# A new order of the opening: k by arrival, the first norm on ScalarE, q in pairs, four divisions and most weight remainders on VectorE

## The chip, the cores and the metric

One core of one Trainium2 chip. The metric is the time of one execution on the device in microseconds (us); lower is better. TensorE is called PE in the profile (its weight loads PEld), VectorE DVE, ScalarE ACT, GpSimd POOL, SyncE SP.

## What is computed

A gated cross-attention block followed by a mixture of experts, in float32. Shapes: x and ctx (4, 512, 256); 16 heads of 64; a window of 65 keys; 2 shared and 16 routed experts of width 128, the best 4 routed ones counted.

```
x = x + tanh(g_xattn) * attention(layernorm(x), ctx, ctx)
x = x + tanh(g_ffn)   * experts(layernorm(x))

attention: q = rope(layernorm(x) @ wq.T); k = rope(ctx @ wk.T); v = ctx @ wv.T
           s = q k^T / 8, masked to i-64 <= j <= i; softmax(s) v; @ wo.T
experts:   gate = top 4 of softmax(x @ router.T)
           sum over experts of gate_e * gelu(x @ up_e.T) @ down_e.T
```

## The kernel before

**Products.** Each float32 operand is split into a high part in the fp32r type and a remainder (`h`, `l`); a product is three matmuls: high by high, high by remainder, remainder by high (`products`, `product`). ScalarE rounds the high part and another engine subtracts it from the source. So each 128x512 piece of weights (`("w", i)`) is loaded to `raw` (4 slots) by SyncE, rounded by ScalarE (L579, semaphore `w_hi`), and its remainder is made either by VectorE (L840, `w_lo_v`), if `i` is in `LO_ON_V`, or by GpSimd (L479, `w_lo_p`). A slot of `raw` is loaded again once both are done (`load_piece`, L338).

**Units.** The attention runs over 16 units (4 batches by 4 groups of 4 heads), `u`, and 64 heads, `c`. For a unit TensorE makes q, k and v (L1009) in one of two pairs of PSUM banks, taken in turn (`ring`): each job takes the pair of the last job but one, and waits until that has been read (`claim`, `released`). q and k are rotated: VectorE shuffles the bank into `swap` (L768) and multiplies the bank by cos (L771); GpSimd multiplies `swap` by sin (L465; L455 for both pairs at once) and adds (L467, L458). A "pair" is half of a unit's q or k, two heads. v goes out through ScalarE (L595).

**Heads.** `scores` (TensorE, L1160, two heads at a time), `score_max` (VectorE, L910), `softmax_numerator` (ScalarE, L628), `invert` (VectorE, the reciprocal of the row sums, L920), `divide` (GpSimd, L471, prob times rinv broadcast, both in SBUF), `transpose_probs` (TensorE, L1172), `copy_transposed` (ScalarE, L637), `values` for two heads (TensorE, L1191), `round_att` (ScalarE, L643) and `rest_att` (VectorE, oTl, L924). When a unit's four heads are done, ("y", u) multiplies by wo and VectorE adds the result to x (L856).

**Order.** All of it is written by hand: each engine has its own queue, a list for the opening (up to head 4) and then a loop over `steps`, one for each head from `OPENED` = 5, with the same jobs on every engine. Engines meet only through semaphores. In the opening VectorE makes the statistics of the first layer norm (L730 to L737) and norms the four tiles of x itself (`normalise_first`, L742); GpSimd makes `rstd` (L490), and only for later norms also `shift`, which ScalarE's `normalise` (L618) needs. k0 waits for both parts of ctx before each half. q of unit 0 is rotated by pairs, q of later units in one piece; VectorE, before it shuffles a q or k, waits until GpSimd is done with the whole of the last one (`joined`). The PE queue of the opening is k0, xT0 (x turned), v0, q0, k1, scores 0, q1, v1, transposes 0, scores 2, transposes 1, q2, values 0, scores 4. After the attention the experts follow with up and down products, without the parts that the change touches.

## Time and profile before

| | before |
|---|---|
| median of 3 runs | 523.23 us (522.90 to 523.24) |
| the profiled execution | 523.18 us |
| its span in the profile | 521.4 us |
| TensorE busy | 503.8 us, 97% |
| VectorE, ScalarE, GpSimd busy | 357.4, 311.1, 276.1 us |
| granted TensorE clock, mean | 0.999 |

The profile shows one execution. A line of a timeline gives start, duration, engine, source line, operation, tiles written and read, shapes, how many, and in brackets the engine's idle time before it with what ended that. Durations of neighbours on one engine overlap somewhat, so start-to-start times are used for sums. A granted clock of 1.00 is TensorE's level of 2.4 GHz.

### The profile page before, as it was taken

To read this page: it belongs to the slowest core of one execution; us is meant where nothing else is said; L and a number is where in the kernel's file an instruction comes from. 1 tells how busy PE (TensorE), PEld (TensorE's weight loads), DVE (VectorE), ACT (ScalarE), POOL (GpSimd) and SP (SyncE) were. 2 spreads that over 40 slices of the span, in tenths; PEclk is the share of its full clock that TensorE was granted. 3 is DMA by queue.
4 is the path that set the end of the run, shared out by engine and by line. 5 is a ranking of instruction groups with operands and counts; after the bars stand their busy time and mean duration, and the time that the engine had idled before them with its cause. 6 is when DMAs were issued, how large, how long until landed. Compare 5 with 4: busy or idle time off the path is not lost.

```text
span 521.4 us, 12294 instructions
## 1 busy us (share of the span) xinstructions
PE 503.8 (97%) x4394; PEld 422.2 (81%) x4394; DVE 357.4 (69%) x1150; ACT 311.1 (60%) x859; POOL 276.1 (53%) x213
## 2 busy tenths in 40 slices
PE   8888999899999999999999999999999999999996
PEld 4767798799889988888888888867887888788884
DVE  6868868558756577775967575697657665855463
ACT  3468677466676657766675794764546545544442
POOL 3989997788889778987998733541000100000000
PEclk9999999999999999999999999999999999999999
DMA  8352323111031011202221128314911491156021
GB/s 258 98 166 50 81 77 105 55 37 36 4 117 36 13 27 36 59 1 58 58 56 43 37 74 314 88 28 107 301 25 21 127 284 17 24 150 233 1 33 47
DMA packets 47723, 44.12 MB, mean 85 GB/s; under 512 B 29168, under 2 KB 31472, under 8 KB 47664
## 3 DMA queue, kind: packets, MB, share of 16 engines
q1 hardware_dynamic: 47664, 43.35, 29.2%
q8 instruction: 35, 0.57, 0.4%
q14 instruction: 24, 0.20, 0.1%
HBM read 30.62 MB, written 2.23 MB: 63 GB/s over the span
## 4 chain that ended last, share of the span: by engine, by line
PE 72%; POOL 10%; DVE 9%; issue 5%; ACT 2%; DMA 1%; SPq 0%; DVEq 0%; POOLq 0%; ACTq 0%
PE ring L1009 50%; PE psS L1009 8%; PE psO L1191 5%; PE psS L1160 4%; PE psT L1172 4%; POOL arena L465 3%; POOL arena L467 2%; POOL prob L471 2%; DVE arena L768 2%; POOL wl L479 1%; POOL arena L458 1%; DVE prob L819 1%; DMA craw<-in_ctx 1%; DVE wl L840 1%; DVE arena L910 1%
## 5 line engine op out<-in xcount | busy, mean ns | idle before, releaser
L1009 PE MATMUL ring<-xTh,wh 128*128 128x512 f32 x272 | 109.7, 403 | 3.0 <-DVE wl L840 1.4
L1009 PE MATMUL ring<-xTh,wl 128*128 128x512 f32 x272 | 106.8, 393 | 0.0
L1009 PE MATMUL ring<-xTl,wh 128*128 128x512 f32 x272 | 106.7, 392 | 0.0
L471 POOL TENSOR_TENSOR prob<-prob,rinv 128x512 f32<-128x512 f32 x64 | 68.0, 1063 | 15.5 <-DVE rinv L920 15.5
L566 ACT ACTIVATE oTh<-prob 128x512 fp32r<-128x512 f32 x64 | 40.4, 632 | 58.0 <-PE ring L1009 26.5
L827 DVE TENSOR_TENSOR oTl<-prob,oTh 128x512 fp32r<-128x512 f32 x64 | 46.3, 724 | 39.4 <-ACT oTh L566 39.1
L1009 PEld LDWEIGHTS ring<-xTh,wh 128*128 128x128 f32 x272 | 51.1, 188 | 16.6 <-issue 4.4
L819 DVE TENSOR_TENSOR prob<-sneg,arena 128x512 f32<-128x512 f32 x64 | 47.4, 740 | 21.6 <-ACT sneg L550 21.6
L637 ACT ACTIVATE pT<-psT 128x512 f32<-128x512 f32 x64 | 38.0, 593 | 40.3 <-PE psT L1172 40.3
L550 ACT ACTIVATE sneg<-ring 128x512 f32<-128x512 f32 x72 | 42.8, 595 | 32.0 <-PE ring L1009 31.9
L1009 PEld LDWEIGHTS ring<-xTh,wl 128*128 128x128 f32 x272 | 51.0, 188 | 11.3
L1009 PEld LDWEIGHTS ring<-xTl,wh 128*128 128x128 f32 x272 | 51.2, 188 | 10.6
L628 ACT ACTIVATE prob<-arena,nmax 128x128 f32<-128x128 f32 x128 | 49.8, 394 | 10.6 <-DVE nmax L910 10.6
L628 ACT ACTIVATE prob<-sneg,nmax 128x128 f32<-128x128 f32 x128 | 49.5, 391 | 9.9 <-DVE nmax L910 9.9
L467 POOL TENSOR_TENSOR arena<-arena 128x512 f32<-128x512 f32 x36 | 47.3, 1313 | 2.8
L465 POOL TENSOR_TENSOR arena<-arena,sin 128x512 f32<-128x512 f32 x36 | 47.4, 1318 | 1.3 <-DVE arena L768 1.3
L455 POOL TENSOR_TENSOR arena<-arena,sin 128x1024 f32<-128x1024 f32 x14 | 34.0, 2428 | 25.1 <-DVE arena L768 25.1
L768 DVE STREAM_SHUFFLE arena<-ring 128x512 f32<-128x512 f32 (+1 forms) x49 | 45.3, 924 | 0.2
L479 POOL TENSOR_TENSOR wl<-raw,wh 128x512 fp32r<-128x512 f32 x22 | 30.9, 1404 | 26.7 <-ACT wh L579 26.6
L1172 PE MATMUL psT<-ident,prob 128*128 128x128 f32 x256 | 39.0, 274 | 5.0 <-POOL prob L471 5.0
L490 POOL TENSOR_TENSOR rstd<-vare,mhalf 128x4 f32<-128x4 f32 x8 | 9.2, 1155 | 63.0 <-DVE vare L737 63.0
L771 DVE TENSOR_TENSOR arena<-ring,cos 128x512 f32<-128x512 f32 (+1 forms) x49 | 40.9, 835 | 0.0
(123 smaller groups left out, 1226.2 us busy)
## 6 DMA issues: line engine op xcount, KB each, us to landing
arena<-gate_scratch SPq DMA_DIRECT2D x64, 256.0 KB, 6.4
raw<-in_e SPq DMA_DIRECT2D x18, 256.0 KB, 2.7
raw<-in_w SPq DMA_DIRECT2D x16, 256.0 KB, 3.6
arena<-arena SPq DMA_DIRECT2D x16, 256.0 KB, 3.1
arena<-arena SPq DMA_DIRECT2D x16, 192.0 KB, 3.4
pT<-pT SPq DMA_DIRECT2D x96, 32.0 KB, 2.0
out<-x SPq DMA_DIRECT2D x16, 128.0 KB, 6.2
x<-in_x SPq DMA_DIRECT2D x3, 512.0 KB, 3.8
```

Source lines behind the costliest of these rows:

```text
L465: link(pool.tensor_tensor(part, part, sin[:, :], ALU.mult))
L467: pool.tensor_tensor(dst, dst, part, ALU.add).then_inc(qk_rot[i], 1)
L471: pool.tensor_tensor(prob[:, c % BUFS, :, :], prob[:, c % BUFS, :, :], rinv[:, c % BUFS, :].unsqueeze(2).to_broadcast([P, TT, P]), ALU.mul ...
L550: act.activation(act_g[:, n % 2, :], ring[0][:, n % 2, :], ACT.Gelu).then_inc(f_gelu, 1)
L566: act.activation(gated_parts(n)[0], src, ACT.Copy).then_inc(f_hi, 1)
L628: last = act.activation(prob[:, c % BUFS, t, :], sneg[c % BUFS][:, t, :], ACT.Exp, bias=nmax[:, c % 4, t:t + 1], scale=-1.0, accum_out=rsu ...
L768: dve.stream_shuffle(swap[:, i, pairs, :], part, [(lane + QUAD // 2) % QUAD for lane in range(QUAD)]).then_inc(qk_swap[i], 1)
L771: dve.tensor_tensor(dst[:, pairs, :], part, cos[:, :].unsqueeze(1).to_broadcast(part.shape), ALU.mult).then_inc(qk_mul[i], 1)
L819: dve.tensor_tensor(act_f[:, n % 4, :], act_g[:, n % 2, :], gate_bc[:, r, :], ALU.mult).then_inc(f_mul, 1)
L827: dve.tensor_tensor(lo, src, hi.bitcast(F32), ALU.subtract).then_inc(f_lo, 1)
L1009: last = pe.matmul(out, a, b, start=start and i == 0 and j == 0, stop=stop and i == n - 1 and j == 2, skip_group_check=check)
L1172: last = pe.transpose(psT[:, t, :], prob[:, c % BUFS, t, :], ident[:, :])
```

## The change

The opening's queues are rewritten; the loop over `steps` stays as it is but for three things: which weight remainders lie on VectorE, that q is rotated by pairs up to unit 2 (`SPLIT_Q`), and that head 4's reciprocal and division move into the opening.

- k0 (`first_keys`): products come in the order in which their inputs arrive: high ctx of part 0 by both halves' weights, then weights' remainder, ctx's remainder, then part 1.
- The first layer norm goes through ScalarE's `normalise` behind weight 1; `normalise_first` is gone, and GpSimd makes `shift` for it too.
- Divisions of heads 0 to 3 run on VectorE (`divide` in the vector block, new semaphore `s_norm_v`).
- Remainders of weights 1, 3, 5, 9, 11, 13, 15 go from GpSimd to VectorE, those of 2 and 6 from VectorE to GpSimd.
- VectorE waits per pair for GpSimd (`rotated` in place of `joined`).
- TensorE: scores 2 before v1, q2 before transposes 1, scores 4 before values 0.

```diff
--- before.py
+++ after.py
@@ -46,7 +46,9 @@
...
-LO_ON_V = (0, 2, 4, 6, 7, 8, 10, 12, 14, 16, 18, 20)
+LO_ON_V = (0, 1, 3, 4, 5, 7, 8, 9, 10, 11, 12, 13, 14, 15, 16, 18, 20)
+DIVIDED_ON_V = 4
+SPLIT_Q = 3
@@ -166,7 +168,7 @@
...
-        s_inv, s_norm = sem("s_inv"), sem("s_norm")
+        s_inv, s_norm, s_norm_v = sem("s_inv"), sem("s_norm"), sem("s_norm_v")
@@ -265,19 +267,19 @@
...
+        def normed(c):
+
+            if c < DIVIDED_ON_V:
+                return s_norm_v, c + 1
+            return s_norm, c + 1 - DIVIDED_ON_V
+
         def rotated(kind, u, pair=1):
 
-            if kind == "k":
-                return 2 * u + pair + 1
-            return pair + 1 if u == 0 else u + 2
-
-        def joined(kind, u, pair=1):
-
-            return 2 * u + pair + 1 if kind == "k" or u < 2 else u + 3
+            return 2 * u + pair + 1 if kind == "k" or u < SPLIT_Q else u + SPLIT_Q + 1
...
-            if kind == "k" or u == 0:
+            if kind == "k" or u < SPLIT_Q:
@@ -367,8 +369,8 @@
...
-                        sp.wait_ge(qk_rot[0], joined("q", UNITS - 1))
-                        sp.wait_ge(qk_rot[1], joined("k", UNITS - 1))
+                        sp.wait_ge(qk_rot[0], rotated("q", UNITS - 1))
+                        sp.wait_ge(qk_rot[1], rotated("k", UNITS - 1))
@@ -487,37 +489,32 @@
...
-                    power = pool.tensor_tensor(rstd[:, :], vare[:, :], mhalf[:, :], ALU.pow)
-                    if n == 0:
-                        power.then_inc(ln_rstd, 1)
-                        return
-                    link(power)
+                    link(pool.tensor_tensor(rstd[:, :], vare[:, :], mhalf[:, :], ALU.pow))
...
-            do(("w", 1))
+            do(("w", 2))
             pool.wait_ge(in_sin, 16)
             rotate_pair(1, 0, 0)
-            do(("w", 3))
...
-            do(("w", 5))
-            divide(0)
+            do(("w", 6))
             rotate_pair(1, 1, 0)
-            divide(1)
+            rotate_pair(1, 1, 1)
             rotate_pair(0, 1, 0)
             rotate_pair(0, 1, 1)
-            divide(2)
-            rotate_pair(1, 1, 1)
-            divide(3)
+            rotate_pair(0, 2, 0)
+            divide(4)
+            rotate_pair(0, 2, 1)
             for c, jobs in steps:
                 u, k = divmod(c, G)
-                if k == 1 and u + 1 < UNITS:
+                if k == 1 and SPLIT_Q <= u + 1 < UNITS:
...
-                divide(c - 1)
+                if c > OPENED:
+                    divide(c - 1)
@@ -611,7 +608,8 @@
...
-                act.wait_ge(xT_pe, min(j, B + 2))
+                if j:
+                    act.wait_ge(xT_pe, min(j, B + 2))
@@ -642,8 +640,8 @@
...
-            for job in (("w", 0), ("ctx", 0), ("w", 1), ("xT", 0), ("w", 2), ("w", 3), ("w", 4), ("w", 5),
-                        ("v", 0), ("w", 6)):
+            for job in (("w", 0), ("ctx", 0), ("w", 1), ("norm_a", 0), ("norm_b", 0), ("w", 2), ("w", 3), ("xT", 0),
+                        ("w", 4), ("w", 5), ("v", 0), ("w", 6)):
@@ -653,9 +651,9 @@
...
-            copy_transposed(1)
             softmax_numerator(2)
             softmax_numerator(3)
+            copy_transposed(1)
@@ -732,17 +730,8 @@
...
-                if j:
-                    dve.tensor_scalar(nmean[:, :], mv[:, :, 0], -1.0, None, ALU.mult)
+                dve.tensor_scalar(nmean[:, :], mv[:, :, 0], -1.0, None, ALU.mult)
                 dve.tensor_scalar(vare[:, :], mv[:, :, 1], EPS, None, ALU.add).then_inc(ln_stat, 1)
-
-            def normalise_first(half):
-                dve.wait_ge(ln_rstd, 1)
-                for t in range(2 * half, 2 * half + 2):
-                    last = dve.tensor_scalar(xn[:, t, :], x[:, 0, t, :], mv[:, t, 0:1],
-                                             rstd[:, t:t + 1], ALU.subtract, ALU.mult)
-                if half:
-                    last.then_inc(ln_norm, 1)
@@ -755,8 +744,6 @@
...
-                else:
-                    dve.wait_ge(qk_rot[i], joined(kind, u - 1))
@@ -764,7 +751,9 @@
...
-                    dve.wait_ge(qk_pe[i], rotated("q", u, pairs.start) if u == 0 else u + 2)
+                    if u:
+                        dve.wait_ge(qk_rot[i], rotated(kind, u - 1, pairs.stop - 1))
+                    dve.wait_ge(qk_pe[i], pairs.start + 1 if u == 0 else u + 2)
@@ -916,8 +905,14 @@
...
-                    dve.wait_ge(s_norm, c - BUFS + 1)
+                    dve.wait_ge(*normed(c - BUFS))
                 dve.reciprocal(rinv[:, c % BUFS, :], rsum[:, c % BUFS, :]).then_inc(s_inv, 1)
+
+            def divide(c):
+                dve.wait_ge(s_inv, c + 1)
+                dve.tensor_tensor(prob[:, c % BUFS, :, :], prob[:, c % BUFS, :, :],
+                                  rinv[:, c % BUFS, :].unsqueeze(2).to_broadcast([P, TT, P]),
+                                  ALU.mult).then_inc(s_norm_v, 1)
@@ -927,32 +922,39 @@
...
-            normalise_first(0)
             rest_ctx(1)
-            normalise_first(1)
+            do(("w", 1))
...
-            do(("w", 2))
+            do(("w", 3))
             do(("w", 4))
-            rotate(("q", 0))
+            rotate(("q", 0), 0)
+            rotate(("q", 0), 1)
...
+            do(("w", 5))
             rotate(("k", 1), 1)
             invert(0)
-            rotate(("q", 1))
+            divide(0)
+            rotate(("q", 1), 0)
             invert(1)
-            do(("w", 6))
+            divide(1)
             score_max(2)
             score_max(3)
+            rotate(("q", 1), 1)
             invert(2)
+            divide(2)
             do(("w", 7))
             invert(3)
-            rest_att(0)
+            divide(3)
             score_max(4)
             score_max(5)
-            rotate(("q", 2))
+            rest_att(0)
+            rotate(("q", 2), 0)
+            invert(4)
+            rotate(("q", 2), 1)
@@ -962,7 +964,7 @@
...
-                if c < CLOSING - 1:
+                if OPENED < c < CLOSING - 1:
@@ -1101,17 +1103,15 @@
...
-                    elif n:
+                    else:
...
-                            if (kind, n, half) == ("k", 0, 0):
-                                pe.wait_ge(c_lo, kc + 1)
...
-                        if n == 0 or half:
+                        if (kind, n) == ("q", 0) or half:
@@ -1146,11 +1146,32 @@
...
+            def first_keys():
+
+                two = banks(("k", 0))
+                pe.wait_ge(w_hi, 1)
+                for kc in range(KC):
+                    hi, lo = xTh[1][:, kc, :], xTl[1][:, kc, :]
+                    pe.wait_ge(c_hi, kc + 1)
+                    for half in range(2):
+                        wide, rest = cols(0, kc * D + half * P, P)
+                        pe.matmul(two[half], wide, hi, start=kc == 0, stop=False)
+                        if (kc, half) == (0, 0):
+                            wait_w_lo(pe, 0)
+                        pe.matmul(two[half], rest, hi, start=False, stop=False)
+                        if kc:
+                            pe.wait_ge(c_lo, kc + 1)
+                            pe.matmul(two[half], wide, lo, start=False, stop=True).then_inc(qk_pe[1], 1)
+                    if kc == 0:
+                        pe.wait_ge(c_lo, 1)
+                        for half in range(2):
+                            pe.matmul(two[half], cols(0, half * P, P)[0], lo, start=False, stop=False)
+
...
-                pe.wait_ge(qk_rot[0], joined("q", u, h // 2))
-                pe.wait_ge(qk_rot[1], joined("k", u, h // 2))
+                pe.wait_ge(qk_rot[0], rotated("q", u, h // 2))
+                pe.wait_ge(qk_rot[1], rotated("k", u, h // 2))
@@ -1165,7 +1186,7 @@
...
-                pe.wait_ge(s_norm, c + 1)
+                pe.wait_ge(*normed(c))
@@ -1196,20 +1217,20 @@
...
-            do(("k", 0))
+            first_keys()
...
+            scores(2)
             do(("v", 1))
             transpose_probs(0)
-            scores(2)
+            do(("q", 2))
             transpose_probs(1)
-            do(("q", 2))
+            scores(4)
             values(0)
-            scores(4)
...

```

## Rows read from the trace of the kernel before

**Rows 1.** The head of the page and its part 1: busy time, share, instructions.

```profile
span 521.4 us, 12294 instructions
PE 503.8 (97%) x4394; PEld 422.2 (81%) x4394; DVE 357.4 (69%) x1150; ACT 311.1 (60%) x859; POOL 276.1 (53%) x213
```

**Rows 2.** Stretches: length, busy us by engine (instructions), granted clock, DMA share, GB/s.

```profile
10.00:60.00 50.00, 44.22 (x466) 36.97 (x465) 39.71 (x143) 29.38 (x100) 46.21 (x36) 1.00 0.40 111
10.00:100.00 90.00, 82.14 (x911) 69.91 (x910) 68.41 (x244) 55.76 (x187) 80.52 (x60) 1.00 0.34 99
100.00:180.00 80.00, 80.00 (x981) 71.40 (x980) 56.07 (x231) 51.95 (x182) 66.32 (x48) 1.00 0.14 38
518.00:521.40 3.40, 0.00 (x0) 0.00 (x0) 0.87 (x3) 0.00 (x0) 0.00 (x0) 0.78 0.46 154
```

**Rows 3.** The chain of waits, 0 to 75 us: its shares by line.

```profile
by line: POOL arena L465 16.5%; issue 14.9%; POOL arena L467 13.6%; PE ring L1009 8.2%; POOL prob L471 8.1%; DMA craw<-in_ctx 6.3%; POOL wl L479 5.0%; POOL arena L458 3.2%; DVE arena L768 3.1%; DVE xn L742 2.8%; DVE arena L771 2.4%; ACT pro
```

**Rows 4.** Timeline of TensorE: starts of k0, q0, scores 0, v1, q2, scores 4, y0, k5.

```profile
8.40 0.47 PE L1009 MATMUL ring<-xTh,wh 128*128 128x512 f32 x1 [0.98 <-DVE xTl L750]
...
17.09 0.47 PE L1009 MATMUL ring<-xTh,wh 128*128 128x512 f32 x1 [1.45 <-DVE wl L840]
...
22.74 1.10 PE L1160 MATMUL psS<-arena 64*64 64x128 f32 x32
...
27.23 0.39 PE L1009 MATMUL ring<-wh,xTh 128*128 128x256 f32 x1 [0.40 <-DVE arena L771]
...
32.88 0.48 PE L1009 MATMUL ring<-xTh,wh 128*128 128x512 f32 x1
...
36.91 1.10 PE L1160 MATMUL psS<-arena 64*64 64x128 f32 x32
...
50.42 0.36 PE L1009 MATMUL ring<-wh,oTh 128*128 128x256 f32 x1 [0.77 <-POOL wl L479]
...
99.59 0.48 PE L1009 MATMUL ring<-xTh,wh 128*128 128x512 f32 x1
```

**Rows 5.** L840 to 110 us (ns min/median/max), and its meetings with GpSimd.

```profile
L840 DVE TENSOR_TENSOR wl<-raw,wh x9: 665/1400/2878, 6.7 to 76.4; 128x512 fp32r<-128x512 f32 x9
...
29.62 0.67 DVE L840 TENSOR_TENSOR wl<-raw,wh 128x512 fp32r<-128x512 f32 x1
...
35.43 1.40 DVE L840 TENSOR_TENSOR wl<-raw,wh 128x512 fp32r<-128x512 f32 x1
...
76.35 2.88 DVE L840 TENSOR_TENSOR wl<-raw,wh 128x512 fp32r<-128x512 f32 x1 [1.25 <-ACT wh L579]
...
29.72 1.70 POOL L467 TENSOR_TENSOR arena<-arena 128x512 f32<-128x512 f32 x1
...
34.98 1.29 POOL L465 TENSOR_TENSOR arena<-arena,sin 128x512 f32<-128x512 f32 x1
36.35 1.60 POOL L467 TENSOR_TENSOR arena<-arena 128x512 f32<-128x512 f32 x1
...
76.29 2.39 POOL L484 TENSOR_TENSOR xTl<-craw,xTh 128x1024 fp32r<-128x1024 f32 x1
```

**Rows 6.** Timeline of VectorE: first of eight maxima, shuffle, multiply, reciprocal.

```profile
24.18 0.28 DVE L910 CUSTOM_DVE_ANT_0 sneg<-psS,mask 128x128 f32<-128x128 f32 x1
...
25.87 0.75 DVE L768 STREAM_SHUFFLE arena<-ring 128x512 f32<-128x512 f32 x1
26.50 0.68 DVE L771 TENSOR_TENSOR arena<-ring,cos 128x512 f32<-128x512 f32 x1
27.10 0.17 DVE L920 RECIPROCAL rinv<-rsum 128x4 f32<-128x4 f32 x1
```

**Rows 7.** Timeline of ScalarE: two tiles of the second norm.

```profile
59.73 1.08 ACT L618 ACTIVATE xn<-x,shift,rstd 128x256 f32<-128x256 f32 x2
```

**Rows 8.** Timeline of the weight loads in the warm-up.

```profile
3.18 0.34 PEld L1026 LDWEIGHTS psS<-arena 128*128 128x128 f32 x1 [0.52 <-issue]
...
5.11 0.19 PEld L1026 LDWEIGHTS psS<-arena 128*128 128x128 f32 x1 [0.24 <-issue]
```

## The prediction

> **What bounds the kernel now.** First the page's head: TensorE is busy 504 of 521 us [rows 1], so only its idle time can be won. The stretches then say where that lies [rows 2]: between 10 and 100 us TensorE is busy 82.1 of 90, between 100 and 180 us 80.0 of 80. So 7.9 us of idle time stand between 10 and 100 us, and with 0.8 that k0 could start earlier (below) it is the most that a change of the opening can bring, and whatever shift the opening has at 100 us stays to the end, since the queues behind it are the same. Third, the chain of waits of the first 75 us [rows 3]: it runs mostly over GpSimd (rotation halves L465 and L467, divisions L471, weight remainders L479), and GpSimd is busy 46.2 of the 50 us from 10 to 60, VectorE 39.7 [rows 2]. Fourth, TensorE's idle moments in order of time [rows 4]: the longest, 1.45 us, is q0's wait for a weight remainder of VectorE; 0.40 is v1's wait for k1's second multiply (L771). The change takes work from GpSimd and gives it to VectorE, so the question is what VectorE's work costs there.
>
> **The price of a VectorE instruction with both inputs in SBUF.** The remainder L840 takes 0.67 us at 29.62, where GpSimd's next instruction starts after it; that one takes 1.70 instead of 1.29. At 35.43 it meets a GpSimd instruction that began at 34.98 and ends at 36.27, and takes 1.40; at 76.35 it meets one that ends at 78.68, and takes 2.88 [rows 5]. In both it ends 0.55 after GpSimd's instruction: the one that starts second stands until the first is done. Over the nine L840 before 110 us the median is 1.40 [rows 5]. While GpSimd is busy without a gap, such an instruction costs VectorE 0.67 to 1.9 us (GpSimd's longest half is 1.3) and costs GpSimd some 0.4. The divisions have never run on VectorE. Bounds: 0.60 start to start like a multiply with the sum in PSUM [rows 6] as low end, 1.9 as high end; I take the price of L840, because prob and rinv lie both in SBUF like raw and wh. The Trainium skill (SBUF — State Buffer, section "Who interferes with whom") says that a VectorE instruction with two SBUF inputs contends with a GpSimd instruction that reads SBUF and that issue order decides who blocks; by that the division pays as L840 does, and it speaks against this change. The rows on L840 agree; no row shows a division there.
>
> **Part by part.** I walk the new queues with start-to-start times: shuffle 0.63, multiply 0.60, two heads of maxima 1.69, reciprocal 0.09 [rows 6], rotation half on GpSimd 1.37 (34.98 to 36.35) and 1.29 [rows 5], two normed tiles on ScalarE about 1.0 [rows 7], q or k on TensorE 2.9 and scores or values 1.05 each (32.88 to 36.91, where q2 and values(0) lie between), and some 0.1 between engines (v1 at 27.23 follows 0.05 behind the multiply that ends at 27.18 [rows 4, 6]). The same walk of the old queues gives q2 at 32.9 and y0 at 50.5, where the trace has 32.88 and 50.42 [rows 4].
>
> *k by arrival, and the first norm on ScalarE.* k0 starts on the first half of ctx without its remainder, at 7.6 instead of 8.40 [rows 4]; its 12 matmuls end at 10.4. VectorE loses four norm instructions. ScalarE does them after weight 1, 9.0 to 10.9 (2x1.0), so x turns at 10.9 (before 11.73), v0 starts at 11.9, and its 24 products end at 15. The copy of x waits behind weights 2 and 3 (to 13.7), the remainder ends at 15.05: q0 at 15.1 instead of 17.09 [rows 4]. **Lead 2.0.**
>
> *GpSimd's order.* Its first job is now the remainder of weight 2, which waits for ScalarE behind the norm: it starts at 11.8, after 4.6 us without work. 11.8+1.25, two pairs of k0 (5.2), two stalls of some 0.5 by VectorE's weights 3 and 4, the first pair of q0 (2.6): scores(0) at 21.8, before 22.74 [rows 4]. **Lead 0.9.** TensorE waits 1.0 for it.
>
> *VectorE from 23 us.* q1 runs 22.9 to 25.8, scores(2) behind it. v1 needs k1's second multiply. VectorE: maxima 23.0 to 24.7, weight 5 (0.67 and a wait of 0.75, GpSimd has no gap then) to 26.1, shuffle and multiply to 27.4: v1 at 27.45, before 27.23. **Lead gone, 0.2 behind.** q2 takes the bank pair of q1, so it needs q1's second multiply, which now stands behind: reciprocal, division 0 (0.67+1.0) to 29.2, first pair of q1 to 30.4, reciprocal, division 1 (0.67+1.0) to 32.3, two maxima to 34.0, shuffle and multiply to 35.2. q2 at 35.3, before 32.88: 2.4 behind, with TensorE idle for 4.4 us. Queued behind that wait on TensorE are the transposes of head 1, scores(4) and values(0). Scores(2) and one transpose were done or moved, so scores(4) comes at 38.6 (before 36.91): **1.7 behind.** GpSimd meanwhile runs dry (37.8 to 43); its four divisions gone from it (4.0 us) bring nothing.
>
> *Up to y0.* y0 needs oTl of pair 1 (L924). VectorE without a gap from scores(4): maxima 1.7 from 39.8, oTl 0.6, q2 by pairs and a reciprocal 2.6, weight 8 (1.4), k2 2.5, weight 9 (1.7, before on GpSimd), maxima 1.7, reciprocal, oTl: 52.7. y0 at 52.75 against 50.42 [rows 4]: **2.3 behind**; about 1 of it is given back behind y0, where a division no longer comes late from GpSimd.
>
> *Weights 9, 11, 13, 15.* They leave GpSimd (1.29 each), which has no use for it any more, and join VectorE among the statistics, y0's sum (L856) and the maxima. By the walk the maxima of head 8 start at 60.7, and TensorE waits for ScalarE's copies and exponentials behind them: 1.6 around scores(10), 1.9 before y1, 1.9 around y2, together 5.4 where the old kernel has 2.1 between 60 and 100 us (7.86 less 5.78 [rows 2]). k5 starts at 103.6 against 99.59 [rows 4]. SyncE's loads come one to three us later with the remainders that free their slots, and weight 10 and later ones are not yet needed; cost nothing, cover the lead of one unit. The pairwise rotation of q2 adds two small starts (0.2, in the sum).
>
> **Sum:** 4.0 us at 100 us, kept to the end. The profiled execution took 523.18 us (span 521.4 [rows 1] and 1.8 around it), the median is 523.23: 523.2+4.0 = 527.2. Varying the durations by 1% and the gaps between engines from 0.05 to 0.12 moves this shift between 3.3 and 5.8.
>
> **Rivals.** (1) *The waits between VectorE and GpSimd are short.* Had every moved instruction the luck of 29.62 (first start), the same walk gives q2 at 31.8, y0 at 47.4 and k5 at 92.7, that is 516.3; with half the waits 520.6, with three quarters of them 523.7. For it: GpSimd has fewer jobs after the change and would leave gaps. Against: from 13 to 37 us its queue has none in my walk. It decides at one point: whether q1's second multiply ends before about 33.2. (2) *Clock.* The granted clock is 1.00 in all stretches with TensorE's idle moments up to 1.45 us, and 0.78 in the last 3.4 us, where TensorE did nothing [rows 2]. In the warm-up a weight load took 0.34 at the low level and 0.19 at the high one, and the loads came 0.86 and 0.43 apart [rows 8]. If the 4.4 us gap before q2 lets the clock fall, q2 takes 2.9 us longer, and scores(4), on which VectorE waits, with it: 530.1. The Trainium skill (TensorE: Matmul & The Clock Gate, section "What's actually happening") says that the default is the throttled level of 1.2 GHz and that activity releases 2.4; it makes this rival possible, and this trace shows such a fall only at its end. (3) *The change shows nothing of its order,* because other waits take over in 60 to 96 us: within 0.2% of before, 523.2; for it speaks only that losses and gains cross zero at three quarters of the waits.
>
> **How the numbers follow.** Forecast 0.55 (its own range 525 to 529), clock 0.10 (530.1), short waits 0.28 (516.3 to 521), same 0.07 (I can tell 0.2%, 1.05 us, from no change, and no less). Slower 0.65, same 0.07, faster 0.28. The range goes from 519.6, which leaves out the better part of rival 1 (0.13), to 530.3.
>
> **What would show it.** Right: q0 some 2 us earlier; TensorE idle 3 to 5 us before q2 on L771; L840 and the new divisions on VectorE at a mean over 1.3 us before 60 us; GpSimd idle before 11 and around 40 us; y0 on L924. Wrong: divisions at 0.7 us, q2 before 33.2, k5 before 99.6. A fallen clock would stand in the granted clock from 31 to 40 us.

## The result, and the profile after

The changed kernel takes 529.84 us (median of 4 runs, 529.52 to 530.77) against 523.07 for the kernel before on the same chip (522.82 to 523.24): ratio 1.0132 [1.0117, 1.0147], 6.8 us slower. The forecast was 527.2 with a range of its own from 525 to 529, which the measured time lies above. For the case that the clock fell before q2 it was 530.1, and that is what happened: the queue of VectorE delayed y0 by what was forecast, and the clock fell on top of it, twice.

The head of the page of the changed kernel, answering [rows 1]; its profiled execution took 529.52 us:

```profile
span 527.6 us, 12322 instructions
PE 507.4 (96%) x4394; PEld 426.1 (81%) x4394; DVE 368.0 (70%) x1162; ACT 312.8 (59%) x863; POOL 269.0 (51%) x207
```

TensorE has the same 4394 matmuls and is busy 3.6 us longer with them: it has run slower somewhere. The stretches of the changed kernel, answering [rows 2] (length, then busy us of TensorE, weight loads, VectorE, ScalarE, GpSimd, each with its instructions; granted clock, DMA share, GB/s), with four short ones in which the clock was not 1.00:

```profile
10.00:60.00 50.00, 41.78 (x387) 35.67 (x385) 42.56 (x125) 26.44 (x90) 39.04 (x29) 0.90 0.40 110
60.00:100.00 40.00, 36.63 (x440) 32.16 (x439) 32.61 (x111) 27.38 (x89) 31.21 (x22) 1.00 0.28 82
100.00:180.00 80.00, 80.00 (x969) 70.82 (x967) 55.16 (x226) 51.70 (x181) 63.77 (x48) 1.00 0.15 41
...
33.00:35.00 2.00, 0.00 (x0) 0.00 (x0) 2.00 (x13) 1.95 (x11) 1.92 (x3) 0.84 0.77 201
35.00:41.00 6.00, 5.86 (x15) 4.60 (x16) 3.85 (x6) 1.23 (x7) 2.48 (x2) 0.50 0.20 46
...
54.00:55.00 1.00, 0.00 (x0) 0.00 (x0) 1.00 (x8) 1.00 (x7) 0.92 (x2) 0.92 0.68 240
55.00:58.00 3.00, 2.60 (x12) 2.63 (x13) 1.37 (x2) 3.00 (x10) 2.92 (x4) 0.50 0.21 47
```

Behind 100 us TensorE is busy 80.00 of 80, as before: everything lies ahead of that. GpSimd is busy 39.0 of the first 50 us (46.2 before), VectorE 42.6 (39.7): the work moved, and TensorE's 44.2 fell to 41.8. In 35 to 41 and in 55 to 58 us the granted clock is 0.50, the level of 1.2 GHz.

TensorE's timeline in the changed kernel, answering [rows 4]: starts of k0, q0, scores 0, v1, q2, scores 4, y0, scores 8, k5:

```profile
8.14 0.80 PE L1158 MATMUL ring<-xTh,wh 128*128 128x512 f32 x1
...
15.05 0.40 PE L1011 MATMUL ring<-xTh,wh 128*128 128x512 f32 x1
...
21.72 1.10 PE L1181 MATMUL psS<-arena 64*64 64x128 f32 x32 [1.04 <-POOL arena L469]
...
27.37 0.39 PE L1011 MATMUL ring<-wh,xTh 128*128 128x256 f32 x1 [0.53 <-DVE arena L760]
...
35.14 0.79 PE L1011 MATMUL ring<-xTh,wh 128*128 128x512 f32 x1 [4.18 <-DVE arena L760]
35.73 0.63 PE L1011 MATMUL ring<-xTl,wh 128*128 128x512 f32 x1
36.16 0.63 PE L1011 MATMUL ring<-xTh,wl 128*128 128x512 f32 x1
...
41.33 1.10 PE L1181 MATMUL psS<-arena 64*64 64x128 f32 x32
...
55.40 0.55 PE L1011 MATMUL ring<-wh,oTh 128*128 128x256 f32 x1 [2.47 <-DVE oTl L919]
...
60.14 1.10 PE L1181 MATMUL psS<-arena 64*64 64x128 f32 x32
...
105.72 0.48 PE L1011 MATMUL ring<-xTh,wh 128*128 128x512 f32 x1
```

q0 is 2.0 us earlier than before, scores 0 is 1.0 earlier, v1 0.1 later, q2 2.3 later, y0 5.0 later, k5 6.1 later. The matmuls of q2 stand 0.43 apart, where those of q0 stand 0.23 apart in the same profile at the full clock (15.05, 15.29, 15.52).

What held q2 is on VectorE. Its timeline in the changed kernel, where the multiply of q1's second pair (L760) is the last line but one:

```profile
24.57 1.51 DVE L829 TENSOR_TENSOR wl<-raw,wh 128x512 fp32r<-128x512 f32 x1
...
27.44 1.69 DVE L913 TENSOR_TENSOR prob<-prob,rinv 128x512 f32<-128x512 f32 x1
29.06 0.74 DVE L757 STREAM_SHUFFLE arena<-ring 128x512 f32<-128x512 f32 x1
...
30.48 1.69 DVE L913 TENSOR_TENSOR prob<-prob,rinv 128x512 f32<-128x512 f32 x1
...
34.42 0.67 DVE L760 TENSOR_TENSOR arena<-ring,cos 128x512 f32<-128x512 f32 x1
...
38.23 0.69 DVE L913 TENSOR_TENSOR prob<-prob,rinv 128x512 f32<-128x512 f32 x1
```

and GpSimd's timeline beside it:

```profile
27.29 1.29 POOL L469 TENSOR_TENSOR arena<-arena 128x512 f32<-128x512 f32 x1
28.54 1.74 POOL L467 TENSOR_TENSOR arena<-arena,sin 128x512 f32<-128x512 f32 x1
...
35.95 1.61 POOL L469 TENSOR_TENSOR arena<-arena 128x512 f32<-128x512 f32 x1
45.63 1.30 POOL L467 TENSOR_TENSOR arena<-arena,sin 128x512 f32<-128x512 f32 x1 [8.07 <-DVE arena L757]
```

Division 0 starts 0.15 after a GpSimd half and ends at 29.13, 0.55 after that half (27.29+1.29 = 28.58), the distance of [rows 5]. Division 3 at 38.23 finds GpSimd idle and takes 0.69.

### The profile page after: what moved, and what is told of

The parts are those of the page before. It is cut to its first block, busy times and chain, and to the rows that moved or that the text cites. A ratio compares the mean times of both kernels' runs of the same rounds, so it can differ in the third digit from the quotient of the medians.

```text
span 527.6 us, 12322 instructions
## 1 busy us (share of the span) xinstructions
PE 507.4 (96%) x4394; PEld 426.1 (81%) x4394; DVE 368.0 (70%) x1162; ACT 312.8 (59%) x863; POOL 269.0 (51%) x207
## 4 chain that ended last, share of the span: by engine, by line
PE 74%; DVE 15%; issue 6%; ACT 3%; POOL 2%; DVEq 0%; ACTq 0%; POOLq 0%
PE ring L1011 51%; PE psS L1011 8%; PE psO L1212 4%; PE psS L1181 4%; PE psT L1193 4%; DVE wl L829 3%; DVE arena L757 2%; DVE arena L760 2%; PE psS L1028 1%; DVE arena L899 1%; DVE sneg L899 1%; DVE prob L808 1%; ACT prob L626 1%; DVE oTl L816 1%; DVE oTl L919 1%
## 5 line engine op out<-in xcount | busy, mean ns | idle before, releaser
L473 POOL TENSOR_TENSOR prob<-prob,rinv 128x512 f32<-128x512 f32 x60 | 64.7, 1078 | 16.8 <-DVE rinv L909 16.8
L547 ACT ACTIVATE sneg<-ring 128x512 f32<-128x512 f32 x72 | 42.9, 595 | 32.0 <-PE ring L1011 31.9
L467 POOL TENSOR_TENSOR arena<-arena,sin 128x512 f32<-128x512 f32 x38 | 51.6, 1359 | 8.1 <-DVE arena L757 8.1
L469 POOL TENSOR_TENSOR arena<-arena 128x512 f32<-128x512 f32 x38 | 49.7, 1307 | 3.0
L757 DVE STREAM_SHUFFLE arena<-ring 128x512 f32<-128x512 f32 (+1 forms) x51 | 45.6, 893 | 0.2
L457 POOL TENSOR_TENSOR arena<-arena,sin 128x1024 f32<-128x1024 f32 x13 | 31.1, 2389 | 26.0 <-DVE arena L757 26.0
L1011 PE MATMUL ring<-wh,oTh 128*128 128x256 f32 x128 | 38.1, 298 | 5.9 <-DVE oTl L919 3.8
L760 DVE TENSOR_TENSOR arena<-ring,cos 128x512 f32<-128x512 f32 (+1 forms) x51 | 41.2, 807 | 0.0
L845 DVE SCALAR_TENSOR_TENSOR x<-ring,tg,x 128x1024 f32<-128x1024 f32 x16 | 20.5, 1280 | 28.5 <-PE ring L1011 28.5
```

Of the source, the lines that this page charges most:

```text
L467: link(pool.tensor_tensor(part, part, sin[:, :], ALU.mult))
L469: pool.tensor_tensor(dst, dst, part, ALU.add).then_inc(qk_rot[i], 1)
L473: pool.tensor_tensor(prob[:, c % BUFS, :, :], prob[:, c % BUFS, :, :], rinv[:, c % BUFS, :].unsqueeze(2).to_broadcast([P, TT, P]), ALU.mul ...
L547: act.activation(act_g[:, n % 2, :], ring[0][:, n % 2, :], ACT.Gelu).then_inc(f_gelu, 1)
L757: dve.stream_shuffle(swap[:, i, pairs, :], part, [(lane + QUAD // 2) % QUAD for lane in range(QUAD)]).then_inc(qk_swap[i], 1)
L760: dve.tensor_tensor(dst[:, pairs, :], part, cos[:, :].unsqueeze(1).to_broadcast(part.shape), ALU.mult).then_inc(qk_mul[i], 1)
```

## Experiments

All of them start from the changed kernel unless another is named; times are medians, ratios are to the kernel before on the same chip, whose median was 522.9 to 523.5. In brackets behind a time stands the lowest and highest of its 4 to 11 executions.

**The clock, by filling the gap before q2.** Four matmuls on zeros into a bank that nobody reads yet, so that TensorE isn't idle:

```diff
             transpose_probs(0)
+            fill(psO[:, :], 4)
             do(("q", 2))
```

> As e1, with the 4 idle matmuls before q2 alone. Theory A: the first fall of the clock costs most: scores(4) 2.8 us earlier, y0 some 2.5 us earlier, its gap is still 2.5 us and the clock still falls there, which costs 1.2 us less what VectorE hides: 527.5 to 528.6. Rival B: 529.5 or more.

Measured: 527.38 us (526.48 to 529.37), ratio 1.0091 [1.0065, 1.0116], 2.5 less than the changed kernel. q2 starts at 34.88, as late as before the fill, and scores 4 3.35 later instead of 6.19. So the half clock of q2 costs 2.84 by the trace, and the wait itself is the rest. The gap before y0 stayed 2.49, and the clock fell behind it to 0.50 from 54 to 57 us. The median is 0.1 below the range of theory A.

**Both gaps.** The same, and two more ahead of y0:

```diff
+                    if n == 0:
+                        fill(two[0], 2)
                     pe.wait_ge(oT_lo, 2 * (n + 1))
```

> The changed kernel, with 4 idle matmuls into psO in TensorE's gap before q2 and 2 into y0's own bank pair in the gap before y0; nothing else. Theory A (the changed kernel's 529.8 us are the forecast shift of 4 us by VectorE's queue, plus the clock at its low level from 34.4 to 41.1 and from 54.8 to 58.1 us): q2 stays at 35.1, its 12 matmuls take 2.8 instead of 5.3 us, scores(4) start at 38.5 instead of 41.3, granted clock 1.00 from 35 to 60 us, time 527 to 527.6. Rival B (the low clock is hidden behind VectorE, and the walk was short for another reason): same clock of 1.00, but time 529.5 or more.

Measured: 528.57 us (526.29 to 529.73), ratio 1.0103 [1.0071, 1.0134], between the ranges of the two theories. TensorE's timeline (q2, scores 4, y0) and three stretches of this kernel:

```profile
34.47 0.50 PE L1011 MATMUL ring<-xTh,wh 128*128 128x512 f32 x1 [0.79 <-DVE arena L760]
...
37.83 1.10 PE L1187 MATMUL psS<-arena 64*64 64x128 f32 x32
...
51.80 0.39 PE L1011 MATMUL ring<-wh,oTh 128*128 128x256 f32 x1 [0.31 <-DVE oTl L919]
...
50.00:60.00 10.00, 9.69 (x107) 7.75 (x106) 8.30 (x32) 6.82 (x22) 8.38 (x8) 1.00 0.38 100
...
60.00:100.00 40.00, 35.57 (x418) 31.22 (x419) 30.93 (x104) 26.24 (x87) 31.30 (x21) 0.96 0.28 84
90.00:95.00 5.00, 3.37 (x22) 2.96 (x21) 3.42 (x20) 3.23 (x12) 4.92 (x5) 0.86 0.15 52
```

The clock is whole through both old gaps, and then it fell behind 90 us, where the two waits that are marked just before are only 0.74 and 0.89 us (one of 1.79 before y1, at 73.61, was followed by no fall). The four executions were 526.29 us at a mean granted clock of 1.000, then 527.47 at 0.997, 529.67 at 0.994 and 529.73 at 0.992. The one at 1.000 gives the price of the order alone, as far as one execution can: 526.29 less 522.93 is 3.4 us. By that the rest of the 6.8, 3.4 us, goes with the clock. The second fill shows no gain on top of the first: the median is 1.2 above that with one fill, and the ranges overlap.

**q1's second pair first.** One edit on VectorE: the multiply on which q2 waits goes ahead of division 1 and the maxima of heads 2 and 3.

```diff
             invert(1)
+            rotate(("q", 1), 1)
             divide(1)
             score_max(2)
             score_max(3)
-            rotate(("q", 1), 1)
```

> The changed kernel, with VectorE's rotation of q1's second pair put ahead of division 1 and the maxima of heads 2 and 3. Theory A (q2 waits for this multiply in VectorE's order, and behind it the whole of VectorE's queue is the bound): q2 at 31.9 instead of 35.1, the clock stays at 1.00 there, but y0 comes only about 0.6 us earlier than the walk's 52.75, at 52.1, after a gap of 3 us in which the clock falls: time 526.5 to 528. Rival C (the gap before q2 alone was the loss): q2's 3.3 us come through in full and with the clock's 2.5 the time is near 524.

Measured: 526.79 us (526.08 to 527.59), ratio 1.0075 [1.0057, 1.0093]: 3.0 us back by moving two instructions. q2 starts at 31.60, but y0 still at 51.73 behind a gap of 2.78, and the clock from 53 to 57 us is 0.65. The fastest two executions are 526.08 at a mean clock of 0.996, the profiled one with this fall, and 526.11 at 1.000: here the fall behind y0 shows no cost in the time.

**The weights back on GpSimd.** Remainders 9, 11, 13 and 15 leave VectorE:

```diff
-LO_ON_V = (0, 1, 3, 4, 5, 7, 8, 9, 10, 11, 12, 13, 14, 15, 16, 18, 20)
+LO_ON_V = (0, 1, 3, 4, 5, 7, 8, 10, 12, 14, 16, 18, 20)
```

> The changed kernel, with the remainders of weights 9, 11, 13 and 15 back on GpSimd as before the change; the opening as changed. Theory A (VectorE is the bound from 40 to 95 us, and these four cost 2.8 us of the 4.0): y0's gap shrinks from 2.5 to about 1 us, its clock does not fall, k5 starts 2.8 us earlier: 525.5 to 527. Rival D (they are hidden, the loss is all in the first 40 us): 529 or more.

Measured: 525.62 us (525.17 to 526.37), ratio 1.0049 [1.0032, 1.0066]: 4.2 us back. TensorE's timeline (q2, y0, scores 8) and one stretch:

```profile
34.61 0.80 PE L1011 MATMUL ring<-xTh,wh 128*128 128x512 f32 x1 [4.22 <-DVE arena L760]
...
53.34 0.36 PE L1011 MATMUL ring<-wh,oTh 128*128 128x256 f32 x1 [0.93 <-DVE oTl L919]
...
57.78 1.10 PE L1181 MATMUL psS<-arena 64*64 64x128 f32 x32
...
35.00:40.00 5.00, 5.00 (x13) 3.74 (x13) 3.37 (x4) 0.70 (x4) 1.96 (x2) 0.50 0.17 53
```

The gap before q2 and its half clock are there as in the changed kernel; q2 itself is 0.53 earlier, with a start of k0 at 7.90 instead of 8.14 and scores 0 at 21.18 instead of 21.72. The gap before y0 fell from 2.47 to 0.93, since weight 9's remainder (1.67 us at 51.23 in the changed kernel) no longer stands before the maxima and oTl, and with it went the second fall of the clock.

**Both edits together.** The last two edits in one kernel.

> e3 and e4 together: q1's second pair before division 1, and weights 9, 11, 13 and 15 back on GpSimd; divisions 0 to 3 on VectorE. Theory A: no gap over 2 us on TensorE, clock 1.00 throughout, k5 0.4 us later than in the kernel before: 523.2 to 524.2, so the two edits give back nearly all of the 6.8 us. Rival G (their gains overlap): above 525.

Measured: 523.24 us (522.65 to 523.98, 10 executions), ratio 1.0004 [0.9995, 1.0013]. The two give back the whole loss, with the divisions still on VectorE. What was lost was lost at two places of one queue. The time was forecast, the clock wasn't. TensorE's values 0 and a stretch of this kernel:

```profile
37.52 1.63 PE L1221 MATMUL psO<-pT,arena 128*64 128x64 f32 x32 [1.66 <-ACT pT L635]
...
35.00:41.00 6.00, 4.34 (x71) 3.79 (x64) 5.45 (x24) 4.80 (x21) 1.57 (x2) 0.75 0.18 48
```

Behind a wait of 1.66 us the clock was 0.50 from 38 to 41 us in this execution, which took 522.98 us all the same, and y0 came at 49.87, before the 50.42 of the kernel before.

**The divisions back on GpSimd.** In GpSimd's list, and out of VectorE's:

```diff
-DIVIDED_ON_V = 4
+DIVIDED_ON_V = 0
...
             rotate_pair(1, 1, 0)
+            divide(0)
             rotate_pair(1, 1, 1)
+            divide(1)
             rotate_pair(0, 1, 0)
             rotate_pair(0, 1, 1)
+            divide(2)
+            divide(3)
```

> The changed kernel, with the divisions of heads 0 to 3 back on GpSimd, between the rotations of k1 and q1 there; weights and order else as changed. Theory A (a division costs VectorE 1.7 us while GpSimd works without a gap, and q1's second multiply stands behind two of them): q2 at 31.8 instead of 35.1, no fall of the clock before it; by the walk of the queues y0 at 50.6 and k5 1.7 us later than in the kernel before: 524.5 to 526. Rival E (the divisions are not what is late, but the order): 528 or more.

Measured: 526.77 us (524.53 to 527.44), ratio 1.0056 [1.0036, 1.0075]. The median lies above the range of theory A; one execution, at a mean clock of 0.999, took 524.53. q2 starts at 31.53, scores 4 waits 1.05 for GpSimd's rotation and the transposes behind it 1.39 for a division, and y0 comes at 50.27, as in the kernel before. The opening is whole again, and what is left of the loss stands behind y0: k5 starts at 103.62, 4.0 later than before, and in this profile the clock fell twice there, from 73 to 77 us behind a wait of 1.78 and from 93 to 98 us behind waits of 0.76 and 0.89. The kernel with both edits has y0 at 49.87 with the divisions on VectorE. So moving the divisions was no mistake by itself; their place was.

**Does the division wait for GpSimd?** The multiplications by sin of unit 1 on GpSimd are left out, so its queue has holes:

```diff
                 pool.wait_ge(qk_swap[i], rotated("qk"[i], n, pair))
-                link(pool.tensor_tensor(part, part, sin[:, :], ALU.mult))
+                if n != 1:
+                    link(pool.tensor_tensor(part, part, sin[:, :], ALU.mult))
```

> The changed kernel without the multiplications by sin of k1 and q1 on GpSimd (the halves with L467 for unit 1), so that part of the computation is left out; GpSimd then stands still for some 40% of the time from 24 to 37 us. Theory (VectorE's divisions are long because of GpSimd's instructions): the first divisions fall to between 0.7 and 1.3 us each and q2 starts at 32.5 to 34 instead of 35.14. Rival (the division is a long instruction on VectorE by itself, and 0.69 at 38.23 was the exception): they stay at 1.5 to 1.7 and q2 at 35.0 or later.

Measured: one execution, 524.95 us. VectorE's first two divisions and TensorE's q2 and y0:

```profile
27.79 0.69 DVE L914 TENSOR_TENSOR prob<-prob,rinv 128x512 f32<-128x512 f32 x1
...
29.83 0.69 DVE L914 TENSOR_TENSOR prob<-prob,rinv 128x512 f32<-128x512 f32 x1
...
33.48 0.50 PE L1012 MATMUL ring<-xTh,wh 128*128 128x512 f32 x1 [2.19 <-DVE arena L761]
...
50.91 0.36 PE L1012 MATMUL ring<-wh,oTh 128*128 128x256 f32 x1 [2.48 <-DVE oTl L920]
54.39 1.10 PE L1182 MATMUL psS<-arena 64*64 64x128 f32 x32
```

0.69 instead of 1.69, twice, with nothing changed on VectorE: the other us is the wait for GpSimd. What the holes change is who starts first: GpSimd's next half starts 0.02 behind division 0 (27.81), and it is that half that takes 1.82 instead of 1.30. q2 comes 1.66 earlier. The granted clock was 1.00 throughout, behind gaps of 2.19 and 2.48 us.

**A division with one SBUF tensor.** If two SBUF inputs of full size are the reason, four instructions with one tensor and a number per partition should be free of it:

```diff
-                dve.tensor_tensor(prob[:, c % BUFS, :, :], prob[:, c % BUFS, :, :],
-                                  rinv[:, c % BUFS, :].unsqueeze(2).to_broadcast([P, TT, P]),
-                                  ALU.mult).then_inc(s_norm_v, 1)
+                for t in range(TT):
+                    last = dve.tensor_scalar(prob[:, c % BUFS, t, :], prob[:, c % BUFS, t, :],
+                                             rinv[:, c % BUFS, t:t + 1], None, ALU.mult)
+                last.then_inc(s_norm_v, 1)
```

> The changed kernel, but each of the four divisions on VectorE is four instructions of 128x128 with one SBUF tensor and one number per partition, instead of one of 128x512 with two SBUF tensors. Theory (a division costs 1.69 us only because it has two SBUF inputs while GpSimd works; 0.69 alone): the four pieces take 0.17 to 0.25 each (the nearest row is the 128x4 instruction of 0.17), 0.7 to 1.0 a division in place of 1.69, so that the first three save some 2 us: q2 at 33.0 to 33.6 instead of 35.14, and 526.5 to 528.5 us. Rival (any VectorE instruction that reads SBUF stands while GpSimd works): each of the four pieces waits, a division costs 1.7 us or more, q2 at 35 or later, 529.5 us or more.

Measured: 533.2 us (531.2 to 535.14), ratio 1.0184 [1.0143, 1.0226]; my theory fell and the rival stands. VectorE's divisions 0 and 3 (four pieces in one line each), TensorE's q2, and two stretches:

```profile
28.22 3.90 DVE L914 TENSOR_SCALAR prob<-prob,rinv 128x128 f32<-128x128 f32 x4
...
41.91 0.88 DVE L914 TENSOR_SCALAR prob<-prob,rinv 128x128 f32<-128x128 f32 x4
...
38.76 0.80 PE L1012 MATMUL ring<-xTh,wh 128*128 128x512 f32 x1 [5.93 <-DVE arena L760]
...
33.00:38.00 5.00, 0.00 (x0) 0.00 (x0) 4.96 (x24) 1.79 (x8) 2.44 (x2) 0.76 0.67 157
...
39.00:44.00 5.00, 5.00 (x21) 3.85 (x24) 3.75 (x10) 0.92 (x7) 1.82 (x2) 0.66 0.21 52
```

3.90 us for what took 1.69, while GpSimd started three halves (28.08, 29.32, 30.71); 2.34 and 2.36 for divisions 1 and 2, and 0.88 for division 3, which finds GpSimd idle. So one tensor in SBUF is enough to meet GpSimd, and four short instructions can meet it more often than one long one. The kernel before had shown it already in its first norm, the same operation on pieces of 128x256: two of them took 0.73 with GpSimd idle, and

```profile
9.42 1.70 DVE L742 TENSOR_SCALAR xn<-x,mv,rstd 128x256 f32<-128x256 f32 x2
```

beside GpSimd's weight remainder, which ran from 9.09 to 10.65. The Trainium skill (SBUF — State Buffer, section "Who interferes with whom") says that an instruction of VectorE with at most one SBUF input doesn't contend unless it runs in a mode with two ports, and that `tensor_scalar` can enter such a mode; the rows fit the second half of the rule, though no run shows in which mode the pieces ran, and the first half alone would have misled here.

**The front by itself.** The kernel before, with only k0 by arrival, the first norm on ScalarE and weight 1's remainder on VectorE (lists of GpSimd, ScalarE, VectorE, TensorE):

```diff
-            do(("w", 1))
...
-            for job in (("w", 0), ("ctx", 0), ("w", 1), ("xT", 0), ("w", 2), ("w", 3), ("w", 4), ("w", 5),
+            for job in (("w", 0), ("ctx", 0), ("w", 1), ("norm_a", 0), ("norm_b", 0), ("xT", 0), ("w", 2), ("w", 3), ("w", 4), ("w", 5),
...
-            normalise_first(0)
...
-            normalise_first(1)
+            do(("w", 1))
...
-            do(("k", 0))
+            first_keys()
```

> The kernel before with one part of the change alone: k0 by arrival of its parts, the first layer norm on ScalarE, weight 1's remainder on VectorE. Theory A (this part is sound, and its lead is lost later only because VectorE is given more): by the walk each station from x turned on is 0.8 us earlier and nothing later takes it back: 522.1 to 522.5. Rival F (a lead at the front is always eaten by GpSimd's queue): 522.8 to 523.2.

Measured: 523.00 us (522.45 to 523.09, 11 executions), ratio 0.9997 [0.9988, 1.0006]: nothing that can be told, where my expectation saw a small gain; the time lies in the range of rival F. x turns at 11.31 instead of 11.73, q0 starts at 16.69 instead of 17.09, and scores 16 and k5 are 0.4 earlier too, so in the profile GpSimd's queue didn't eat the lead, but it is half of the 0.8 expected and too small to be told in the time.

**What k0 waits for.** In the profiles of this study k0 starts anywhere from 7.15 to 8.41 us. The weight loads of the warm-up of the changed kernel, answering [rows 8]:

```profile
6.59 0.34 PEld L1028 LDWEIGHTS psS<-arena 128*128 128x128 f32 x1 [0.52 <-issue]
7.26 0.19 PEld L1028 LDWEIGHTS psS<-arena 128*128 128x128 f32 x1 [0.33 <-issue]
```

The clock rose between 6.6 and 7.3 us; in the profile of before it rose by 4.68. TensorE had no idle moment between the last warm-up matmul and k0, so here the warm-up held it. To see whether it always does, one matmul of the five was taken away from the new order below:

```diff
-WARM_UP = 5
+WARM_UP = 4
```

> The new order (518.04 us) with four warm-up matmuls instead of five. In the profiles of this case the granted clock rose to its upper level at some point between 4.7 and 7.3 us, and k0 started at 7.41 where it rose early and at 8.22 where it rose late, since the warm-up matmuls stand ahead of it. Theory (the warm-up is what k0 waits for): with one matmul of the five away k0 starts at 7.3 to 7.5 whenever the clock rises, up to 0.8 us earlier than in the late profiles; of that lead 0.0 to 0.5 us reach the end: 517.5 to 518.1. Rival (without that matmul TensorE stands still before k0, and the clock rises later or falls again): k0's matmuls 0.43 apart instead of 0.23, q0 later than 16.5, 518.5 to 520 us.

Measured: 517.79 us (517.08 to 518.07), ratio 0.9891 [0.9875, 0.9906], the same as with five. The time lies in the theory's range, by luck, since the start of k0 doesn't. ScalarE's rounding of ctx and TensorE's k0 in its profile:

```profile
7.36 1.29 ACT L581 ACTIVATE xTh<-craw 128x512 fp32r<-128x512 f32 x2 [1.33 <-DMA craw<-in_ctx]
...
8.13 0.47 PE L1167 MATMUL ring<-xTh,wh 128*128 128x512 f32 x1 [0.89 <-ACT xTh L581]
```

k0 started at 8.13, not at 7.3 to 7.5: now it was the arrival of ctx that held it. In the profiles ScalarE's first rounding of ctx begins from 6.1 to 7.6 us. So k0 waits for the later of two things, both of which differ by over a us between executions, and the theory that the warm-up is what it waits for is wrong as a rule.

**A better order.** The walk of the queues that the forecast used was corrected by what the runs had shown and used to look for an order. On VectorE:

```diff
-LO_ON_V = (0, 1, 3, 4, 5, 7, 8, 9, 10, 11, 12, 13, 14, 15, 16, 18, 20)
+LO_ON_V = (0, 1, 3, 4, 6, 7, 10, 12, 16, 18, 20)
...
             rotate(("k", 1), 0)
             score_max(0)
-            score_max(1)
-            do(("w", 5))
             rotate(("k", 1), 1)
             invert(0)
+            score_max(1)
             divide(0)
             rotate(("q", 1), 0)
+            rotate(("q", 1), 1)
+            do(("w", 7))
             invert(1)
-            divide(1)
             score_max(2)
             score_max(3)
-            rotate(("q", 1), 1)
+            divide(1)
+            rotate(("q", 2), 0)
```

Division 2 goes behind the maxima of head 4 and division 3 behind those of head 5, GpSimd makes the remainders 2, 5, 8, 9, 11, 13, 14 and 15, TensorE makes v1 and transposes 0 before scores 2 and scores 4 before transposes 1, and ScalarE's list is shifted to match.

> An order of my own on the changed kernel's parts: divisions 0 to 3 on VectorE, weights 2, 5, 8, 9, 11, 13, 14 and 15 on GpSimd, the rotations of q1 ahead of k1's second pair on GpSimd and ahead of division 1 and the maxima on VectorE, division by division spread, v1 before scores(2), scores(4) before the transposes of head 1. By the walk of the queues, with the price of each meeting of VectorE and GpSimd as in the traces, TensorE's longest gap is 1.0 us and k5 starts 6.8 us earlier than in the kernel before: 516.3. Theory A: 515.5 to 518. If the walk is only right for the order it was made for: 520 or more.

Measured: 518.04 us (517.19 to 518.3), ratio 0.9900 [0.9886, 0.9914]: 5 us faster than before and 11.8 faster than the change, at the upper edge of the range of theory A (518). The stretches of this kernel, to be read beside [rows 2]:

```profile
10.00:60.00 50.00, 46.70 (x481) 39.35 (x479) 44.71 (x154) 33.73 (x113) 46.89 (x36) 1.00 0.41 119
10.00:100.00 90.00, 86.02 (x988) 73.99 (x987) 72.08 (x258) 60.40 (x200) 83.63 (x61) 1.00 0.35 101
```

TensorE has 86.0 of 90 us where it had 82.1. Both side engines are busier than before from 10 to 60 us, and no wait of TensorE is over 0.80 between 10 and 100 us. A second order, with two divisions on VectorE and two on GpSimd, against the first (the start of VectorE's list; other remainders and the lists of all engines differ too):

```diff
-DIVIDED_ON_V = 4
+DIVIDED_ON_V = 2
...
             score_max(0)
-            rotate(("k", 1), 1)
-            invert(0)
             score_max(1)
-            divide(0)
+            rotate(("k", 1), 1)
             rotate(("q", 1), 0)
+            invert(0)
             rotate(("q", 1), 1)
-            do(("w", 7))
             invert(1)
+            divide(0)
```

> A second order of the walk: two divisions on VectorE (heads 0 and 1), heads 2 and 3 divided on GpSimd, remainders of weights 2, 6, 9, 13, 14 on GpSimd, q1's second multiply before the first division. Theory (with the order right, TensorE has no gap over 1 us between 10 and 100): q2 before 31.5, scores(16) at 88 to 89.5, 516.5 to 519 us, like the first order. Rival (GpSimd becomes the bound with the two divisions, and the clock falls behind a gap): scores(16) after 91, 521 us or more.

Measured: 518.44 us (518.13 to 518.64), ratio 0.9905 [0.9889, 0.992], q2 at 30.37, scores 16 at 88.99. The two can't be told apart. Since they differ in more than the divisions, this doesn't price a division alone; it shows that an order with two of them on VectorE can be as fast as one with four.

## Why the prediction was right, and where it was not

The measured time lies in the stated range of 519.6 to 530.3, near its upper end. The way and the cause were forecast; the likeliest case, 527.2 with 525 to 529, was missed, because it kept the full clock behind the gap before q2.

**k by arrival and the norm: the lead at the end of k0 was mis-sized.** k0 was to start at 7.6 and end at 10.4; in the trace it starts at 8.14 and x turns at 11.30, a lead of 0.43 instead of 0.8. The 7.6 took ScalarE's rounding of ctx from one execution, and both that and the end of the warm-up move. q0 came at 15.05 all the same (forecast 15.1), but not by the forecast's path, a wait for x's remainder: that ended at 14.79, and TensorE went from k0 to q0 without a gap. v0 started 0.2 late, at 12.10, and took 2.95 instead of 3.1; in the nine profiles with this front's lists q0 stands 2.95 or 2.96 behind v0, at 14.35 in the earliest, so an earlier or later v0 moves it. In the front by itself the 0.4 could be followed to scores 16 in the profile, and couldn't be told from nothing in the time.

**GpSimd's order: right.** Weight 2 started at 11.73 (11.8), scores 0 at 21.72 (21.8).

**VectorE from 23 us: right, and the rival of short waits fell.** Weight 5 took 1.51, divisions 0 and 1 1.69 each (1.67 forecast), v1 came at 27.37 (27.45), q2 at 35.14 (35.3) behind 4.18 us of idle time (4.4). The point from which the short waits would have decided was 33.2; the multiply ended at 35.09. That a division costs 0.69 if GpSimd has holes was shown by the kernel without the sin halves. GpSimd ran dry from 37.6 to 45.6 (37.8 to 43).

**Clock: the rival came on top.** This is the step of the forecast that failed: the 527.2 left the clock at its upper level behind a gap of 4.4 us. The fall had a chance of 0.10, and the time that it gave, 530.1, is within 0.3 of the median. Scores 4 were to come at 38.6, or 2.9 later at the low level; they came at 41.33, 2.7 later. All three kernels with an idle time over 4 us before q2 (the changed one, the one with the weights back, the one with divisions in pieces) fell in it or behind it (0.50, 0.50 and 0.66 in the stretches shown). The Trainium skill (TensorE: Matmul & The Clock Gate, section "What's actually happening") says that the throttled level is the default and activity releases it; the trace agrees, with 0.50 from 35 to 41 us behind the gap of 4.18. By the prediction's own rows such a fall gave 530.1, and I should have given that more than 0.10, since my own forecast held the 4.4 us gap and nothing in the trace of before had a gap over 1.45 inside the work to speak for the clock's staying up. The profile's only long idle stretch, its end, did show a fall [rows 2].

**y0: the step was right, and a second fall was missed that was hidden.** y0 was forecast at 52.75; with the 2.7 of the clock that is 55.45, and it came at 55.40, on oTl. The us that was to be given back behind y0 was there: from y0 to scores 8 is 3.51 at the full clock (the kernel with both gaps filled; 3.48 without the sin halves), where the kernel before took 4.52. But in the changed kernel it took 4.74, because the 2.47 us gap ahead of y0 let the clock fall again. That is 1.2 us of TensorE's which no sentence of the prediction has. But VectorE was the bound there: the maxima of head 8 start 7.73 behind y0 (63.13), 7.83 in the kernel with both gaps filled and 7.71 in the one without the sin halves, which had no fall there. The walk had 7.95. So the second fall was hidden behind VectorE's queue.

**Weights 9 to 15: the mechanism right, TensorE's idle time too large.** TensorE was to lose 5.4 us between 60 and 100 us against 2.1 before; it lost 3.4 (40 less 36.63). The waits before y1 and around y2 were there, 1.73 and 1.64 for 1.9 each, but not the 1.6 around scores 10. In the kernel with both gaps filled waits of 0.75 and 0.27 do stand there, and TensorE loses 4.4 (40 less 35.57 busy): the second fall had used up time that would have been idle. From the maxima of head 8 to k5 the changed kernel takes 42.6 us, the walk had 42.9. Putting weights 9, 11, 13 and 15 back gave 4.2 us (3.15 in the profiled executions). There 2.4 stood at scores 8 (57.78 against 60.14): 0.5 was there at scores 4 already, from an earlier front, 1.6 came at y0 and 0.3 behind it, and another 0.9 behind the maxima of head 8 (41.7 to k5), where the forecast looked for most of it.

**The sum.** At k5 the shift is 6.1, forecast 4.0. (The terms as the prediction prints them, 2.3 less 1 and 5.4 less 2.1, add up to 4.6; the 4.0 is the walk's 103.6 for k5.) In the trace the excess over the walk is 2.65 at y0, 2.4 at the maxima of head 8 and 2.1 at k5. It is the first fall, 2.84 by the experiment with one fill, of which the other engines made up a part. So 530.1, which adds the whole 2.9 to the whole 4.0, comes somewhat by luck within 0.3: the profiled execution is 6.3 longer than that of the kernel before, and the medians differ by 6.8. Without a fall of the clock the order costs 3.4 us (one execution of the kernel with both gaps filled), at the lower end of the 3.3 to 5.8 that the varied durations had given.

## What to carry over

A side engine's queue is priced at its busiest moment: put the instruction on which TensorE waits ahead of those that can meet GpSimd, and move work by its place, not by its engine; here two edits decided over 6.6 us, with the divisions left where they were. Where a forecast holds a gap of several us on TensorE, price the half clock behind it as part of the forecast, and ask at each gap whether another engine's queue hides it: the first fall here is about 2 us of the shift at k5, and the second shows in none of it. A start that waits for a DMA or the warm-up has no fixed time: take its spread over executions before counting tenths of a us of lead.

## What the runs showed of the hardware

- The clock falls behind gaps under 3 us in some cases and not in others: behind 2.47 (the changed kernel), 2.49 (one fill) and 2.78 us (q1 first), and not behind 2.19 and 2.48 (no sin halves), nor behind 2.48 us before y0 in the kernel with divisions in pieces. It fell behind 1.66 us with both edits together and behind 1.78 before y1 with the divisions back on GpSimd, and not behind 1.79 before y1 with both gaps filled. It also fell between 93 and 104 us, behind marked gaps of 0.7 to 0.9, in the profiles of four kernels (one fill, both gaps filled, divisions back, divisions in pieces), and not behind the same two gaps in the changed kernel. What tells these cases apart stays open.
- Executions of one kernel scatter with it: 526.29 to 529.73 us at mean clocks from 1.000 to 0.992, while the front, the first new order and both edits together, at 0.997 or more, keep within 0.6, 1.1 and 1.3 us.
- The rise in the warm-up came from 4.7 us (the kernel before) to 7.4 (both edits together) over the profiles. The Trainium skill (TensorE: Matmul & The Clock Gate, section "What's actually happening") puts the scatter of this point at 500 ns to either side; here it is 1.3, and the measurement decides.
- VectorE's `tensor_scalar` on float32 in SBUF can stand behind GpSimd as a two-input instruction does, piece by piece: 3.90, 2.34 and 2.36 us for four of 128x128 beside GpSimd, 0.88 without it.
